# Attention 0 of a two-layer decoder: scores of four row groups per step, values and output one step sooner, early weight splits on GpSimd, link rows on VectorE

## Reference, cut to what matters

```python
x = x + attn0(layernorm(x))                 # linear attention, 16 heads of 16, below
x = x + 0.6 * sigmoid(si[:, :, None] + sj[:, None, :] + b) + 0.4 * layernorm(x)   # "links": si = ctx @ W[:64], sj = ctx @ W[64:]
x = x + moe0(layernorm(x))                  # 16 experts and a shared one, by chunks of 128 rows
...                                         # layer 1: attention, cross attention, experts
# attn0
q, k, v = silu(x @ Wq), silu(x @ Wk), silu(x @ Wv)
o = (q @ k.T * decay[h]) @ v                # decay[h] = exp(ld[h] * (i - j)) for i >= j, else 0
o = o * sigmoid((x @ Wg1) @ Wg2)
o = o * rsqrt(mean(o * o over the head) + eps) * w
return o @ Wo
```

## Time and profile before

| | |
|---|---|
| median of 3 runs | 936.22 us (930.77, 936.22, 937.33) |
| profiled execution, its time | 944.64 us |
| its span | 942.9 us |
| its mean granted TensorE clock | 0.984 |
| PE, DVE, ACT, POOL busy | 98%, 65%, 45%, 11% |
| attention 0 with its tail | about 15 to 130 us of the span |

### The profile page before, as it was taken

How to read it: one execution, slowest core, us unless ns; L and a number is a source line. 1 busy time by engine, 2 the same in 40 slices (tenths; PEclk the granted TensorE clock), 3 DMA queues, 4 the chain that set the end, 5 groups by cost and what they waited for, 6 DMA issues and landing times.

```text
span 942.9 us, 14229 instructions
## 1 busy us (share of the span) xinstructions
PE 919.3 (98%) x5393; PEld 704.2 (75%) x5393; DVE 613.9 (65%) x1183; ACT 423.9 (45%) x1063; POOL 101.2 (11%) x127
## 2 busy tenths in 40 slices
PE   8999989999999999999999999999999999999998
PEld 5666667888888887666877777777776778888886
DVE  3336965666666667665777778687876666666664
ACT  7235354334334348974443434343445443333442
POOL 3000100000000021000322323232320000000000
PEclk9589999999999999999999999999999999999999
DMA  5001201111110050000620000000001111111001
GB/s 170 0 1 60 78 18 45 53 38 48 50 33 1 1 223 1 2 2 1 257 86 1 1 1 2 1 1 1 2 11 40 35 47 37 51 50 50 17 0 45
DMA packets 12249, 36.80 MB, mean 39 GB/s; under 512 B 1920, under 2 KB 4192, under 8 KB 11424
## 3 DMA queue, kind: packets, MB, share of 16 engines
q1 hardware_dynamic: 12160, 36.02, 11.5%
q0 software_dynamic: 32, 0.01, 0.0%
HBM read 34.98 MB, written 1.05 MB: 38 GB/s over the span
## 4 chain that ended last, share of the span: by engine, by line
PE 86%; DVE 7%; ACT 5%; issue 1%; DMA 1%; SPq 0%; DVEq 0%; ACTq 0%
PE ps L1315 80%; PE ps L1953 3%; PE ps L1495 2%; ACT Q L1107 1%; DVE stats L456 1%; DMA X<-in_x 1%; DVE weighted_h L675 1%; DVE xn L464 0%; ACT probs_q L1222 0%; DVE h_lo L685 0%; DVE X L511 0%; ACT whi L1122 0%; PE ps L1326 0%; ACT silu_g L1147 0%; DVE probs_q L842 0%
## 5 line engine op out<-in xcount | busy, mean ns | idle before, releaser
L1152 ACT ACTIVATE h_hi<-weighted_h 128x512 fp32r<-128x512 f32 x100 | 63.2, 632 | 154.7 <-DVE weighted_h L675 152.6
L685 DVE TENSOR_TENSOR h_lo<-weighted_h,h_hi 128x512 fp32r<-128x512 f32 x100 | 69.2, 692 | 66.5 <-ACT h_hi L1152 66.3
L1315 PE MATMUL ps<-xT_first,whi 128*128 128x512 f32 x376 | 111.3, 397 | 1.2 <-ACT silu_g L1147 1.2
L1315 PE MATMUL ps<-xT_second,whi 128*128 128x512 f32 x376 | 108.5, 391 | 1.3 <-ACT silu_g L1147 1.2
L709 DVE TENSOR_TENSOR shared_gate<-silu_g,row_shares 128x512 f32<-128x512 f32 x88 | 60.8, 691 | 63.4 <-ACT silu_g L1147 63.3
L1147 ACT ACTIVATE silu_g<-ps 128x512 f32<-128x512 f32 x100 | 59.6, 596 | 75.2 <-PE ps L1315 75.0
L1315 PE MATMUL ps<-xT,merged_q 128*128 128x256 f32 x384 | 91.9, 384 | 0.0
L1307 POOL TENSOR_TENSOR latent_rot<-rope_buf 128x256 f32<-128x256 f32 x96 | 68.5, 735 | 180.0 <-DVE rope_buf L797 180.0
L1315 PEld LDWEIGHTS ps<-xT_first,whi 128*128 128x128 f32 x376 | 70.4, 188 | 18.9 <-issue 2.8
L1315 PEld LDWEIGHTS ps<-xT_second,whi 128*128 128x128 f32 x376 | 70.1, 188 | 17.0 <-issue 2.5
L1315 PE MATMUL ps<-h_hi,wlo 128*128 128x512 f32 x200 | 78.5, 392 | 0.0
(11 more groups left out here) (196 smaller groups left out, 1593.5 us busy)
## 6 DMA issues: line engine op xcount, KB each, us to landing
raw<-in_ffn SPq DMA_DIRECT2D x50, 384.0 KB, 3.1
wx<-in_wx SPq DMA_DIRECT2D x4, 2048.0 KB, 9.7
cx<-in_cx SPq DMA_DIRECT2D x1, 1536.0 KB, 6.5
X<-in_x SPq DMA_DIRECT2D x4, 256.0 KB, 5.6
kvc<-in_kvc SPq DMA_DIRECT2D x1, 1024.0 KB, 15.1
out<-X SPq DMA_DIRECT2D x4, 256.0 KB, 2.2
wqkv<-in_wqkv SPq DMA_DIRECT2D x1, 768.0 KB, 7.5
wqkv<-in_wqkv SPq DMA_DIRECT2D x1, 512.0 KB, 5.7
```

What stands on the lines that cost most here:

```text
L685: v.tensor_tensor(h_lo[:, u % 2, :], weighted_h[:, u % 2, :], h_hi[:, u % 2, :].bitcast(F32), ALU.subtract).then_inc(act_lo[l], 1)
L1152: a.activation(h_hi[:, u % 2, :], weighted_h[:, u % 2, :], ACT.Copy).then_inc(act_hi[l], 1)
L1315: return pe.matmul(o, l, r, start=start, stop=stop, skip_group_check=True)
```

## The change

A step now holds all four row groups: 12 steps, `scores_by_key(b, k)`, each with four row groups in turn on banks 4 to 7, so the four banks have one owner at a time, and the next step waits for both decay products of the step before. The pieces around the steps are written in another order: values and output of a sequence come one step sooner, the four quarters in one row. `link_rows` moves to DVE (a product, a sum and a scale on new inputs `xb_t`, `xb_r`, loaded behind X). The splits of the first three weight chunks move to GpSimd, between its fourth and fifth addition to the links. The decay table is finished in three parts. The last rows of each engine's list are also in another order. Of the three `attention0` the removed lines are left out here, since the listing above has them.

```diff
-sp.dma_start(xb_b[:, :], d["xb_b"]).then_inc(xb_b_loaded, 16)
...
+sp.dma_start(xb_t[:, :, :], d["xb_t"]).then_inc(xb_b_loaded, 16)
+sp.dma_start(xb_r[:, :], d["xb_r"]).then_inc(xb_b_loaded, 16)
+sp.dma_start(xb_b[:, :], d["xb_b"]).then_inc(xb_b_loaded, 16)
...
-def decayed(n):
+def decayed(b, k):
-    v.wait_ge(pe_s, n + 1)
-    b, half, k = n // 6, n // 3 % 2, n % 3
-    if k == 0:
-        v.tensor_tensor(P1[:, b % 2, 8 * half:8 * half + 8, :], step_scores(n).rearrange("p i (h q) -> p (i h) q", h=4),
-                        DT[:, 8 * half:8 * half + 8, 0:128], ALU.mult).then_inc(p_done, 1)
-    else:
-        v.tensor_tensor(by_group(P0, b, half, k - 1), step_scores(n).rearrange("p i (e q) -> p i e q", e=2),
-                        DT[:, 8 * half:8 * half + 8, :].rearrange("p (i m e) q -> p i m e q", i=2, m=2)[:, :, k - 1], ALU.mult).then_inc(p_done, 1)
+    v.wait_ge(pe_s, 6 * b + 2 * k + 2)
+    for half in range(2):
+        by_key = ps[:, 4 + 2 * half:6 + 2 * half, :]
+        if b == 0 and k == 0:
+            v.wait_ge(dt_ready, 1 + 2 * half)
+        if k == 0:
+            v.tensor_tensor(P1[:, b % 2, 8 * half:8 * half + 8, :], by_key.rearrange("p i (h q) -> p (i h) q", h=4),
+                            DT[:, 8 * half:8 * half + 8, 0:128], ALU.mult).then_inc(p_done, 1)
+        else:
+            v.tensor_tensor(by_group(P0, b, half, k - 1), by_key.rearrange("p i (e q) -> p i e q", e=2),
+                            DT[:, 8 * half:8 * half + 8, :].rearrange("p (i m e) q -> p i m e q", i=2, m=2)[:, :, k - 1], ALU.mult).then_inc(p_done, 1)
+        if b == 0 and k == 0 and half == 0:
+            link_rows()
...
+def link_rows():
+    v.wait_ge(xb_b_loaded, 16 * 3)
+    v.tensor_tensor(xb_p[:, :, :], xb_t[:, :, :], xb_r[:, :].unsqueeze(1).to_broadcast([P, TILES, 64]), ALU.mult).then_inc(xa_products, 1)
+    v.wait_ge(xa_products, 1)
+    v.tensor_reduce(xb_a[:, :], xb_p[:, :, :], AX, ALU.add).then_inc(xa_sums, 1)
+    v.wait_ge(xa_sums, 1)
+    v.tensor_scalar(xb_a[:, :], xb_a[:, :], xb_b[:, 0:1], 0.5, ALU.add, ALU.mult).then_inc(xa_ready, 1)
...
 def attention0():
+    for a in range(NB):
+        b = a - 1
+        decayed(a, 0)
+        if a == 0:
             normalise(0, 2)
+        if a >= 2:
+            add_out(0, a - 2)
+            norm_statistics(1, a - 2)
+        if a >= 1:
+            gated_values(b)
+        decayed(a, 1)
+        if a == 0:
             v.wait_ge(const_loaded, 16)
             v.tensor_copy(identb[:, :], ident).then_inc(setup_v, 1)
             v.tensor_copy(negqs[:, :], neg_qs).then_inc(setup_v, 1)
+            normalise(0, 3)
+        if a == NB - 1:
+            normalise(2, a - 3)
+            normalise(1, a - 2)
+            scaled(0, b)
+        decayed(a, 2)
+        if 1 <= a < NB - 1:
+            scaled(0, b)
+        if a == NB - 2:
+            blocks_output(a - 2)
+    bilinear(NB - 3)
     gated_values(NB - 1)
+    norm_statistics(2, NB - 3)
     add_out(0, NB - 2)
     norm_statistics(1, NB - 2)
+    normalise(2, NB - 3)
+    normalise(1, NB - 2)
     scaled(0, NB - 1)
+    tokens_low(0, 0)
+    bilinear(NB - 2)
+    norm_statistics(2, NB - 2)
     add_out(0, NB - 1)
     norm_statistics(1, NB - 1)
+    normalise(2, NB - 2)
     blocks_output(NB - 1)
+    router_maxima(0, 0)
     normalise(2, NB - 1)
     weight_shared(0, 0)
     weight_shared(0, 1)
     act_low(0, 0, 0)
+    tokens_low(0, 1)
+    router_probabilities(0, 0)
     act_low(0, 1, 1)
+    router_choice(0, 0)
...
 def experts(l):
...
+    if l == 0:
+        v.wait_ge(w_lo[0], EARLY)
...
 def attention0():
     a.preload_act_table_set(LN_EXP)
     norm(0, 0)
     a.wait_ge(first_const, 16)
     a.wait_ge(ld_loaded, 16)
     decay(range(0, 4))
     transposed_tokens(0, 0)
     decay(range(8, 12))
+    decay((4, 5, 12, 13))
     norm(0, 1)
     queries(0)
     keys(0)
     gate_inner(0)
     values(0)
     transposed_tokens(1, 1)
     gate(0)
     a.preload_act_table_set(LN_EXP)
+    decay((6, 7, 14, 15))
     norm(0, 2)
     norm(0, 3)
     for period in range(NB):
         b, c = period - 1, period + 1
+        if period >= 1:
+            gate(period)
         if c == NB:
+            a.preload_act_table_set(LN_EXP)
+            norm(2, period - 3)
+            norm(1, period - 2)
             squares(b)
+            split_hi(0, 0, 0, 0)
+            root(b)
+            split_hi(0, 1, 1, 0)
+            split_hi(0, 2, 2, 0)
         else:
+            if period >= 1:
+                squares(b)
             queries(c)
             keys(c)
             if period == 0:
                 links(0)
+            if period >= 1:
                 a.preload_act_table_set(LN_EXP)
+            if period >= 2:
+                norm(1, period - 2)
+            if period >= 1:
+                root(b)
+            gate_inner(c)
             values(c)
             if period == 0:
                 links(1)
+            if c + 1 < NB:
+                transposed_tokens(c + 1, c + 1)
     spread_rows(0)
     squares(NB - 1)
+    norm(2, NB - 3)
     root(NB - 1)
+    norm(1, NB - 2)
+    tokens_high(0, 0)
+    silu(0, 0, 0)
+    a.preload_act_table_set(LN_EXP)
     norm(2, NB - 2)
+    copy_logits(0, 0)
     norm(1, NB - 1)
     norm(2, NB - 1)
+    logit_exponentials(0, 0)
     silu(0, 1, 1)
     act_high(0, 0, 0)
     silu(0, 2, 2)
+    tokens_high(0, 1)
     act_high(0, 1, 1)
+    copy_logits(0, 1)
...
-for part in range(2):
-    g.wait_ge(dt_exp, HEADS // 2 * (part + 1))
-    diagonal = DT[:, 8 * part:8 * part + 8, 0:128]
-    g.tensor_tensor(diagonal, diagonal, k("causal").unsqueeze(1).to_broadcast([P, 8, 128]), ALU.mult).then_inc(dt_ready, 1)
+for first, last in ((0, 8), (8, 12), (12, 16)):
+    g.wait_ge(dt_exp, last)
+    diagonal = DT[:, first:last, 0:128]
+    g.tensor_tensor(diagonal, diagonal, k("causal").unsqueeze(1).to_broadcast([P, last - first, 128]), ALU.mult).then_inc(dt_ready, 1)
 g.wait_ge(xsig_ready, TILES)
 g.tensor_scalar(xsig[:, :, :], xsig[:, :, :], 0.3, 0.3, ALU.mult, ALU.add).then_inc(xsig_scaled, 1)
 g.wait_ge(xsig_scaled, 1)
 for t in range(TILES):
+    if t == 4:
+        g.wait_ge(pe_last_p0, 1)
+        for c in range(EARLY):
+            g.wait_ge(w_hi[0], c + 1)
+            g.tensor_tensor(wlo[:, c, :], raw[:, c, :], whi_first[:, c, :].bitcast(F32), ALU.subtract).then_inc(w_lo[0], 1)
     g.wait_ge(x_part, t + 1)
...
-        pe.wait_ge(p_done, 6 * b + (5, 6, 4, 4)[quarter])
+        pe.wait_ge(p_done, 6 * b + (4, 6, 2, 2)[quarter])
...
-def scores_by_key(n):
+def scores_by_key(b, k):
-    b, half, k = n // 6, n // 3 % 2, n % 3
-    if n >= 2:
-        pe.wait_ge(p_done, n - 1)
+    if b + k:
+        pe.wait_ge(p_done, 6 * b + 2 * k)
     heads = 4 if k == 0 else 2
-    by_head = step_scores(n).rearrange("p i (h q) -> p i h q", h=heads)
     for h in range(heads):
         m, e = divmod(h, 2) if k == 0 else (k - 1, h)
         kk = (kE, kO)[e]
-        for i in range(2):
-            r = slice(64 * half + 32 * i, 64 * half + 32 * i + 32)
+        for g in range(4):
+            r = slice(32 * g, 32 * g + 32)
+            by_head = ps[:, 4 + g, :].rearrange("p (h q) -> p h q", h=heads)
             if k == 0:
-                last = mm(by_head[:, i, h, :], kk[r, b, m, 128:256], qT[r, b, m, 128:256], True, True)
+                last = mm(by_head[:, h, :], kk[r, b, m, 128:256], qT[r, b, m, 128:256], True, True)
             else:
-                last = mm(by_head[:, i, h, :], kk[r, b, m, 0:128], qT[r, b, m, :], True, True)
-    last.then_inc(pe_s, 1)
+                last = mm(by_head[:, h, :], kk[r, b, m, 0:128], qT[r, b, m, :], True, True)
+    last.then_inc(pe_s, 2)
...
 def attention0():
     zeros_times_zeros()
     pe.wait_ge(first_const, 16)
     transposed_tokens(0, 0)
     pe.wait_ge(wq_loaded, 16)
     queries(0)
     pe.wait_ge(wkv_loaded, 16)
     keys(0)
     values(0)
     pe.wait_ge(wg_loaded, 16 * 2)
     gate_inner(0)
     pe.wait_ge(k_ready, 2)
     transposed_tokens(0, 1)
     gate(0)
+    for a in range(NB):
+        b, c = a - 1, a + 1
+        pe.wait_ge(q_ready, a + 1)
+        pe.wait_ge(k_ready, 2 * a + 2)
+        if a == 0:
             pe.wait_ge(g1_ready, 1)
             pe.wait_ge(v_ready, 2)
+        scores_by_key(a, 0)
+        if a >= 1:
+            gate(a)
+        if a >= 2:
+            output0(a - 2)
+        if a >= 1:
+            for quarter in range(4):
+                mixed_values(b, quarter)
+        if c < NB:
             queries(c)
+        scores_by_key(a, 1)
+        if c < NB:
+            keys(c)
+        else:
+            mixed_values(a, 2)
+            mixed_values(a, 3)
+        if a == 0:
             pe.wait_ge(xb_loaded, 16 * 2)
             links(0)
+        else:
+            sums_of_squares(b)
+        scores_by_key(a, 2)
+        if c < NB:
             gate_inner(c)
             values(c)
+        if a == 0:
+            links(1)
+        if c + 1 < NB:
             pe.wait_ge(g1_ready, c + 1)
```

(27 more changed lines are left out.)

128 lines of the change are left out of this document (21 added, 107 removed).

## The result

The changed kernel takes **925.98 us** (median of 10 runs, 924.6 to 928.81) against 934.38 us for the kernel before beside it (10 runs): a ratio of 0.9913, 95% interval 0.9891 to 0.9936. A second series of the same kernel gave 926.39 us (10 runs) and a ratio of 0.9898. One of the ten runs before, at 951.14 us, was in a slower state with a lower clock that some executions of any kernel show; the ratios leave such runs out, and without it the median before is 932.55 us. The forecast of 920 us was 6 us too low; the range held the time.

The account below looks back on a forecast made before the run. PE was taken to set the pace, half-clocked for 30.72 us, with DVE busy late. From 929.2 at full clock, terms summing to -12.2 gave 917.0; +3 for low clock made 920 us, range 911 to 933.

Parts of the forecast that it names:

- Score steps: Attention on PE: 24 steps become 12 at 1.06 us each with four row groups at once, -12.7 us.
- Two row groups at a time: Rival on the score steps: row groups run only two at once, a step takes 2.1 us, 930 us; chance 0.09.
- Link rows: Sixteen one-column records leave PE for DVE, -1.8 us.
- The new wait: Sequence 0, before the second score step: PE idle from 18.7 to 22.1 us for the decay product, +3.4 us.
- The clock's first stretch: After the wait in sequence 0 the clock falls again, about 6 us at the low level, +3 us.
- The low clock as long as before: Rival on the clock: the low stretch of 30.72 us stays as long, 932 us; chance 0.12.
- The base: The kernel before without its low clock stretch: 944.6 - 15.4 = 929.2 us.
- Splits hidden: Three weight splits on GpSimd, 5.3 to 6.6 us, cost nothing; up to 2 us if high parts come late.
- The tail: Last sequence and tail: PE's waits sum to 6.3 us against 6.7 before, -0.4 us.
- Order on PE: Value quarters in one place per sequence instead of three: 0.15 us saved six times, -0.9 us.
- DVE as the bound: Rival: PE waits for DVE's blocks ahead of product pairs at four places, 8 us, so 928; chance 0.15.
- Slower: Rival: PE's waits bring back the low clock and hold it through attention and tail, 966 us; chance 0.04.

Follow-up runs that it names:

- Experiment 2: The changed kernel with a wait on PE in each score step, between row groups 0 and 1 and row groups 2 and 3: 934.92 us, ratio 0.9996.
- experiment 4: The changed kernel with the link rows back on PE, before sequence 0's second score step, and without the three loads for DVE: 926.11 us, ratio 0.9901.
- the control: The changed kernel a second time, word for word: 926.39 us (10 runs).
- Experiment 5: The changed kernel with the three early weight splits back on DVE at three places of its list, none on GpSimd: 924.22 us, ratio 0.9884.
- experiment 6: The changed kernel with the shared expert's first silu on ACT moved behind the norms and the logit exponentials: 924.82 us, ratio 0.9883.

## Why the prediction was right, and what it had wrong

The direction and the mechanism held, by steps:

- **Score steps, -12.7 us: right in size.** 1.07 us a step against 1.06 forecast. Experiment 2 takes the overlap away and the gain with it. By the figure of the Trainium skill that was cited against it, 3.07 times ("TensorE: Matmul & The Clock Gate", "Measured speedup vs the span model"), a step would take 3.84 / 3.07 = 1.25 us, an estimate from that figure. That is 0.25 more than four at once (1.00), but only 0.19 more than the 1.06 of the sum, so it would have taken 2.3 us off, not 3. The row shows 1.07, 3.6 times.
- **Two row groups at a time, 930 us:** no, as the same row shows. Experiment 2 stands nearest to it, at 935: its step takes 2.27 us and not 2.1, which makes 2 us of the difference, and the base and the clock were low by 3.3 in every time that the prediction gives.
- **Link rows, -1.8: right** (1.7 between runs of 1.000 with and without them). But in the new kernel they would have been free on PE too (experiment 4).
- **The new wait, 18.7 to 22.1, +3.4: right.** 3.49 us, from 19.86 to 23.35; all of it 1.2 us later than forecast, because sequence 1's statistics came at 10.68 us instead of 9.35. That start moves between 8.84 and 10.86 us from profile to profile without regard to the edits. In the control they came at 9.05, and the same wait of 3.49 us ended at 22.28, where the forecast had 22.1. Together with the link rows' -1.8 the wait is one effect, since in this kernel the rows would fit into it.
- **The clock's first stretch, about 6 us: right** for the profiled execution, 6.83. What was missing is the second, 3.41 us at 86.90, behind PE's waits in the tail. I had ruled it out by the earlier trace rows, where a window with 19% idle PE kept 1.00. Over twenty runs the clock costs 0.0060 x 926 x 0.85 = 4.7 us, not 3: **1.7 us of the miss.**
- **The low clock as long as before, 932 us:** no. The profiled execution has 10.2 us at the lower level against 30.7, and the lowest mean clock of the twenty runs is 0.991.
- **The base, 929.2, was 1.6 us low.** I priced the low stretch of the profiled execution of before at half its length, 15.4. At 0.87 us for each us lost it is 13.4 (why not all of it counts isn't shown; that part of it falls into waits is the likely reading), and 944.6 - 13.4 = 931.2; the runs at 1.000 show 930.8.
- **"Splits hidden" is the step that failed.** They are hidden as far as the expert pieces go: nothing waits for a low part. I looked for who waits for GpSimd, and not for what GpSimd takes from DVE. DVE stood 2.0 us, and PE waited 0.75 and 1.13 behind it. Experiment 5 gives back 2.0 us by the medians, 1.4 at full clock. My bound was "up to 2 us", but for another reason.
- **The tail, -0.4 (6.3 us of waits).** By the windows PE stands 0.79 + 2.55 + 3.66 = 7.0 us from 28.87 on, so the sum was near and its parts were not. Squares 1.47 (1.4) came in size. The norm of sequence 1 and the last scaling, forecast at 1.6 and 1.0, came as one wait of 1.73. The one forecast at the third step of the last sequence (1.2) was 0.41. New are 0.75 and 1.13 behind the splits and 0.83 for `vpad` from ACT at 69 us. The table switch that I counted into the small waits costs 1.4 by itself (experiment 6).
- **Order on PE, -0.9: too much.** The earlier trace rows and the next row of that timeline give the values of a sequence before, in three places:

```profile
79.85 1.03 PE L1315 MATMUL ps<-xT,wg 128*16 128x256 f32 x4
```

  1.00 + 1.00 + (79.85 - 78.95) = 2.90 us. Now they stand in one:

```profile
54.65 2.81 PE L1334 MATMUL ps<-P,vpad 128*32 128x256 f32 x64
57.38 1.99 PE L1334 MATMUL ps<-xT,wqkv 128*128 128x256 f32 x8
```

  57.38 - 54.65 = 2.73, so 0.17 a sequence, not 0.3, and 0.5 over three. The fourth sequence went the other way: its 64 records stood in one place (2.78 us from start to start) and now stand in three, about 3.1. Together some -0.2, **0.7 us of the miss.**
- **DVE as the bound, 928 us:** partly. PE is never held for long, but of what the short steps save about 2 us go into waits for DVE and ACT from 69 us on, besides the 2.8 of the wait in sequence 0 (experiment 2). That is this rival's mechanism at a smaller price than its 8, and the splits' 0.75 and 1.13 are among it.
- **Slower, 966 us:** the low level came back, once, for 3.41 us, and wasn't held.
- **The signs.** The last value matmuls ended at 85.9 us (81 forecast) and the second down half at 110.3 (104): the start, the splits' waits and the clock together.

The account: 920 forecast, 1.6 from the base, 1.7 from the clock; the work at full clock fell by 930.8 - 921.7 = 9.1 us, not by 12.2, which is the other 3.1. Of these 1.4 are the splits and some 0.7 the order on PE. The other 1.0 stays open between the waits of the tail and the 1.6 us that came back behind it; no run tells them apart. The later start, about 1 us in the profiled pair, belongs to single executions and doesn't explain the medians.

## What to carry to other kernels

When one engine's steps get shorter, walk the engines beside it through the same stretch before counting the gain: here experiment 2 put 14.4 us on PE, and the time rose by 8.7. A move to an idle engine has two prices, who waits for its result and whom it slows while it runs, and the second one isn't in any chain of waits. Where a few us of clock decide, compare the mean clocks of many runs; a single profile gave 30.7 us at the low level where the mean of 49 runs (0.9949) is about a third of that.
